# Attention scores from three narrower weight products, with the PSUM banks and the order of work rearranged around them

## The reference, cut to what matters

```python
qh = split_heads(x @ wq.T + bq, 16)          # 32 columns per head
kh = split_heads(ctx @ wk.T + bk, 16)        # 77 keys
vh = split_heads(ctx @ wv.T + bv, 16)
scores = einsum('ntd,nsd->nts', qh, kh) / sqrt(32) + mask * PAD
out = merge_heads(einsum('nts,nsd->ntd', softmax(scores), vh)) + x
out = (out - mean(out)) / sqrt(var(out) + 1e-5) * gamma + beta
```

## Time and profile before

| | |
|---|---|
| runs | 1153.67, 1154.09, 1157.71 us, median 1154.09 |
| the profiled execution | 1157.28 us |
| its span, first to last instruction | 1155.5 us |
| mean granted TensorE clock | 0.988 of 2.4 GHz |
| phase two begins | about 132 us |
| one iteration of phase two | 31.2 us, from 531.66 to 562.9 |
| busy: PE, DVE, POOL, ACT | 97%, 71%, 67%, 53% |

### The profile page before, as it was taken

How to read it: one execution, slowest core, us unless ns; L and a number is a source line. 1 busy time by engine, 2 the same in 40 slices (tenths; PEclk the granted TensorE clock), 3 DMA queues, 4 the chain that set the end, 5 groups by cost and what they waited for, 6 DMA issues and landing times.

```text
span 1155.5 us, 25702 instructions
## 1 busy us (share of the span) xinstructions
PE 1123.1 (97%) x7541; PEld 1037.8 (90%) x7541; DVE 822.1 (71%) x1622; ACT 612.5 (53%) x1008; POOL 771.8 (67%) x667
## 2 busy tenths in 40 slices
PE   7899999999999999999999999999999999999994
PEld 7788789999999999999999999999999999999983
DVE  5776467777777777777777777777777777777786
ACT  3321254556566555555555656655555555565551
POOL 4999523677766676766667776667676666777465
PEclk9999999999999999999999999999999999999996
DMA  7745433233343444343344333344443334333223
GB/s 228 261 147 188 150 104 90 74 122 95 116 119 117 126 126 126 116 120 99 102 123 122 106 105 119 117 126 126 126 116 122 98 102 123 123 101 110 85 82 128
DMA packets 147207, 141.07 MB, mean 122 GB/s; under 512 B 86452, under 2 KB 88004, under 8 KB 147172
## 3 DMA queue, kind: packets, MB, share of 16 engines
q1 hardware_dynamic: 146564, 140.29, 40.1%
q10 hardware_dynamic: 608, 0.33, 0.1%
HBM read 91.71 MB, written 48.85 MB: 122 GB/s over the span
## 4 chain that ended last, share of the span: by engine, by line
PE 84%; DVE 2%; POOL 1%; issue 0%; ACT 0%; DMA 0%; DVEq 0%; SPq 0%; POOLq 0%
PE q_ps L724 31%; PE o_ps L765 23%; PE s_ps L740 18%; PE t_ps L751 12%; POOL x_lo L991 0%; DVE stats L822 0%; DVE attn L853 0%; PE q_ps L765 0%; DVE y L862 0%; DMA xT_raw<-in_xT 0%; DVE attn L814 0%; DVE row_max L885 0%; DVE y L868 0%; ACT q_hi L1030 0%; DVE y L843 0%
## 5 line engine op out<-in xcount | busy, mean ns | idle before, releaser
L765 PE MATMUL o_ps<-v_tiles,pt 128*128 128x66 f32 x2520 | 310.7, 270 | 1.5 <-DVE attn L814 1.5
L765 PEld LDWEIGHTS o_ps<-v_tiles,pt 128*128 128x128 f32 x2520 | 304.0, 192 | 1.9 <-issue 1.9
L885 DVE TENSOR_REDUCE row_max<-s_ps 128x8 f32<-128x616 f32 x256 | 203.2, 794 | 118.2 <-PE s_ps L740 118.1
L740 PE MATMUL s_ps<-bd,q_hi 128*128 128x308 f32 x1024 | 260.5, 305 | 1.1 <-ACT q_hi L1030 1.1
L991 POOL TENSOR_TENSOR x_lo<-xT_raw,x_hi 128x512 fp32r<-128x512 f32 x124 | 159.3, 1286 | 117.8 <-ACT x_hi L1026 117.7
L961 POOL TENSOR_TENSOR attn<-attn,x_rows 128x512 f32<-128x512 f32 x124 | 160.2, 1292 | 115.8 <-DVE attn L814 115.8
L1036 ACT COPY pt<-t_ps 128x512 f32<-128x512 f32 (+1 forms) x320 | 175.0, 588 | 107.1 <-PE t_ps L751 107.0
L1030 ACT ACTIVATE q_hi<-q_ps,bq_col 128x512 fp32r<-128x512 f32 x125 | 86.1, 689 | 254.9 <-PE q_ps L724 254.9
L724 PE MATMUL q_ps<-x_lo,wq_hi 128*128 128x512 f32 x500 | 218.7, 437 | 2.5 <-PEq L142 2.1
L1016 ACT ACTIVATE probs<-probs 128x616 f32<-128x616 f32 x256 | 183.3, 716 | 64.3 <-DVE probs L894 64.3
L894 DVE TENSOR_TENSOR probs<-s_ps,row_max 128x616 f32<-128x616 f32 x256 | 204.6, 799 | 5.7
(11 more groups left out here) (96 smaller groups left out, 1292.9 us busy)
## 6 DMA issues: line engine op xcount, KB each, us to landing
xT_raw<-in_xT SPq DMA_DIRECT2D x128, 256.0 KB, 3.5
x_rows<-in_x SPq DMA_DIRECT2D x32, 1024.0 KB, 5.6
out<-y SPq DMA_DIRECT2D x128, 256.0 KB, 2.1
k_scratch<-k_out SPq DMA_DIRECT2D x8, 1232.0 KB, 5.4
bd<-k_scratch SPq DMA_DIRECT2D x128, 77.0 KB, 2.4
v_scratch<-v_out SPq DMA_DIRECT2D x16, 264.0 KB
v_tiles<-v_scratch SPq DMA_DIRECT2D x256, 9.9 KB
ctx_raw<-in_ctxT SPq DMA_DIRECT2D x3, 1232.0 KB, 6.2
```

What stands on the lines that cost most here:

```text
L740: mm = pe.matmul(s_ps[t % 2][:, j, 0:GS], (q_hi, q_lo)[u][:, g, P * t:P * t + P], bd[par][:, v, g, :, :].rearrange("p h s -> p (h s)"), st ...
L765: mm = pe.matmul(bank_of(b, t)[:, col:col + tile_cols[i]], pt[h][0:w, i, P * t:P * t + P], v_tiles[v_buffer(b, h)][0:w, i, 0:tile_cols[i]] ...
L885: dve.tensor_reduce(row_max[:, u, :].rearrange("p (j h) -> p j h", j=2), score_heads(t), AX.X, ALU.max).then_inc(max_ready, 1)
```

## The change

The score block of four heads is split otherwise. A head needs three terms, so four heads have twelve blocks of 32 rows by 77 keys. They are now packed into three weights of four row groups each: `q_a` holds the high part of heads 0, 1, 2 and again of head 0; `q_c` the low part of heads 0, 1, 2 and the high part of head 1; `q_b` the rest, of heads 2 and 3. Each head has 78 columns (77 and one of padding), so `q_a` and `q_c` meet 3 x 78 = 234 columns (`k_ac`), `q_b` 2 x 78 = 156 (`k_b`). There are still six score matmuls in a step. For that:

- Q's high part is two activations of ScalarE (96 and 64 rows), its low part two instructions of VectorE (96 and 32 rows); three DMAs on ScalarE's queue (`move_q`) copy Q's rows to other partitions, once for two groups.
- Keys are loaded by twelve DMAs for each batch, before by four.
- Q is made one step earlier (`q_of_step`) and has two PSUM banks; turns have one bank, and their order is 0 after the scores of tile step 0, 1 before and 2 after those of step 1, 3 and 4 after those of steps 2 and 3.
- VectorE makes Q's low part at the end of a step, in even steps. ScalarE does the exponential first, then Q, copies, x, normalizations. The quarters of x are split in steps 3, 4, 5 and 7.
- In phase one ScalarE copies the first half's keys of chunk 0 before the high part of chunk 1 and the `keep_v` tiles; KS, the number of key buffers, is 5, before 6; `keep_rows` lies in `v_out`. Gamma and beta are loaded at the start of phase two, where VectorE and GpSimd wait for them.

```diff
-    KDMA = HG * DMA
+    KDMA = 3 * HG * DMA
+    QDMA = 3 * DMA
-    KS = 6
+    KS = 5
+    SW = S + 1
+    QW = 3 * DH
...
                 for c in range(CHUNKS):
+                    if c == 0:
+                        keys(0, 0)
                     if c + 1 < CHUNKS:
                         high(c + 1)
-                    keys(c, 0)
+                    if c == 0:
+                        act.wait_ge(keep_turned, 1)
+                        for j in range(VT):
+                            act.copy(keep_v[0:v_n[j], j, :], v_ps[3][0:v_n[j], HEADS * j:HEADS * j + HEADS]
+                                     ).then_inc(keep_v_ready, 1)
+                    else:
+                        keys(c, 0)
...
-            t_ps = [ps(two, f"t_ps{i}", [P, BANK]) for i in range(2)]
-            q_ps = ps(two, "q_ps", [P, BANK])
+            t_ps = ps(two, "t_ps", [P, BANK])
+            q_ps = [ps(two, f"q_ps{i}", [P, BANK]) for i in range(2)]
+            X_STEPS = (3, 4, 5, 7)
-            TURNS = ([], [0, 1], [2, 3], [4])
+            TURNS_AHEAD = ([], [1], [], [])
+            TURNS_BEHIND = ([0], [2], [3], [4])
+            def q_of_step(s):
+                half, u = (s + 1) // 4, (s + 1) % 4
+                return (half + 1) // 2, (0 if half == 1 else 2) + u // 2, u % 2
...
                     at_least(sp, scores_done, b * 8 - 8)
-                    for q in range(HG):
-                        rows = slice(DH * q, DH * q + DH)
-                        sp.dma_start(bd[par][rows, :, :, q, :].bitcast(F32), k_dram[b, rows, :, :, :]
+                    for ac in range(2):
+                        for h in range(3):
+                            rows = slice(DH * h, DH * h + DH)
+                            sp.dma_start(k_ac[par][rows, ac, :, h, 0:S].bitcast(F32), k_dram[b, rows, 0, :, :]
+                                         ).then_inc(k_loaded[par], DMA)
+                        rows = slice(DH * ac, DH * ac + DH)
+                        sp.dma_start(k_ac[par][QW:P, ac, :, ac, 0:S].bitcast(F32), k_dram[b, rows, 1, :, :]
                                      ).then_inc(k_loaded[par], DMA)
+                    for q in range(2):
+                        sp.dma_start(k_b[par][DH * q:DH * q + DH, :, 1, 0:S].bitcast(F32), k_dram[b, QW:P, 0, :, :]
+                                     ).then_inc(k_loaded[par], DMA)
+                        rows = slice(DH * (q + 2), DH * (q + 2) + DH)
+                        sp.dma_start(k_b[par][rows, :, q, 0:S].bitcast(F32), k_dram[b, rows, 1, :, :]
+                                     ).then_inc(k_loaded[par], DMA)
+                sp.dma_start(gamma_all[:], gamma.partition_broadcast(P)).then_inc(scale_loaded, DMA)
+                sp.dma_start(beta_all[:], beta.partition_broadcast(P)).then_inc(scale_loaded, DMA)
...
+                    pe.wait_ge(q_moved[h], (b + 1) * QDMA)
                     for j in range(2):
                         g = 2 * h + j
-                        for n, (u, v) in enumerate(terms):
-                            mm = pe.matmul(s_ps[t % 2][:, j, 0:GS], (q_hi, q_lo)[u][:, g, P * t:P * t + P],
-                                           bd[par][:, v, g, :, :].rearrange("p h s -> p (h s)"),
-                                           start=(n == 0), stop=(n == 2))
+                        for ac, q in ((0, q_a), (1, q_c)):
+                            pe.matmul(s_ps[t % 2][:, j, 0:3 * SW], q[:, g, P * t:P * t + P],
+                                      k_ac[par][:, ac, g, :, :].rearrange("p h s -> p (h s)"),
+                                      start=(ac == 0), stop=False, skip_group_check=True)
+                        mm = pe.matmul(s_ps[t % 2][:, j, 2 * SW:GS], q_b[:, g, P * t:P * t + P],
+                                       k_b[par][:, g, :, :].rearrange("p h s -> p (h s)"),
+                                       start=False, stop=True, skip_group_check=True)
                     mm.then_inc(scores_done, 1)
...
                     pe.wait_ge(exp_done, b * 8 + (4 * h + 4))
-                    at_least(pe, pt_ready, b * (2 * NT) + (NT * h + i - 1))
+                    at_least(pe, pt_ready, b * (2 * NT) + (NT * h + i))
...
                         if real(a):
                             subtract_max(a, h, t)
+                        ahead, g, part = q_of_step(s)
+                        if part == 1 and real(a + ahead) and not in_phase_one(a + ahead, g):
+                            q_low(a + ahead, g)
...
-                        if 3 <= s <= 6 and real(a + 2):
-                            split_x(a + 2, s - 3, par)
+                        if s in X_STEPS and real(a + 2):
+                            split_x(a + 2, X_STEPS.index(s), par)
...
+                def move_q(b, h):
+                    act.wait_ge(q_hi_ready, b * 8 + (4 * h + 4))
+                    g = slice(2 * h, 2 * h + 2)
+                    act.dma_start(q_a[QW:P, g, :].bitcast(F32), q_a[0:DH, g, :].bitcast(F32)).then_inc(q_moved[h], DMA)
+                    act.dma_start(q_c[QW:P, g, :].bitcast(F32), q_a[DH:2 * DH, g, :].bitcast(F32)
+                                  ).then_inc(q_moved[h], DMA)
+                    act.dma_start(q_b[0:DH, g, :].bitcast(F32), q_b[QW:P, g, :].bitcast(F32)).then_inc(q_moved[h], DMA)
```

More of the change, by code:

```diff
@@ L96, in xattn @@
         q_lo_ready = sem("q_lo_ready")
+        q_moved = [sem(f"q_moved_{i}") for i in range(2)]
         x_hi_ready = sem("x_hi_ready")
@@ L251, in _ @@
                 sp.wait_ge(k_loaded[0], KDMA)
-                sp.wait_ge(consts_loaded, 3 * DMA)
+                sp.wait_ge(consts_loaded, DMA)
                 for half in range(2):
@@ L581, in xattn @@
             x_rows = sb(two, "x_rows", [P, TT, D], F32)
+            gamma_all = sb(two, "gamma_all", [P, D], F32)
+            beta_all = sb(two, "beta_all", [P, D], F32)
             attn = [sb(two, f"attn{i}", [P, TT, D], F32) for i in range(2)]
@@ L772, in step @@
                         h, t = s // 4, s % 4
-                        qb = a + h
-                        g = (2 if h == 0 else 0) + t // 2
-                        if real(qb) and not in_phase_one(qb, g):
-                            q_half(qb, g, t % 2, (par + h) % 2)
-                        if real(a):
-                            scores(a, h, t, par)
+                        ahead, g, part = q_of_step(s)
+                        if real(a + ahead) and not in_phase_one(a + ahead, g):
+                            q_half(a + ahead, g, part, (par + ahead) % 2)
                         last_turns = is_last(a - 1) and h == 0
@@ L784, in step @@
                         if real(a - 1 + h):
-                            for i in TURNS[t]:
+                            for i in TURNS_AHEAD[t]:
+                                turn(a - 1 + h, 1 - h, i)
+                        if real(a):
+                            scores(a, h, t, par)
+                        if real(a - 1 + h):
+                            for i in TURNS_BEHIND[t]:
                                 turn(a - 1 + h, 1 - h, i)
@@ L949, in step @@
                             subtract_max(a, h, t)
+                        ahead, g, part = q_of_step(s)
+                        if part == 1 and real(a + ahead) and not in_phase_one(a + ahead, g):
+                            q_low(a + ahead, g)
                         if s == 1 and real(a - 2) and not is_last(a - 2):
                             row_factors(a - 2)
+                dve.wait_ge(scale_loaded, 2 * DMA)
                 steps(dve, step)
@@ L985, in _ @@
                 pool.memset(minus_half[:], -0.5).then_inc(half_set, 1)
+                pool.wait_ge(scale_loaded, 2 * DMA)
                 pool.wait_ge(half_set, 1)
@@ L1035, in copy_pt @@
                     w = tile_rows[i]
-                    act.copy(pt[h][0:w, i, :], t_ps[(NT * h + i) % 2][0:w, :]).then_inc(pt_ready, 1)
+                    act.copy(pt[h][0:w, i, :], t_ps[0:w, :]).then_inc(pt_ready, 1)
                 def norm(b, t, par):
```

139 lines of the change are left out of this document (82 added, 57 removed).

## The result

The changed kernel takes 1284.03 us (median, 1278.2 to 1289.83) beside 1155.89 for the kernel before: ratio 1.111, interval 1.104 to 1.118, 128 us more. Forecast: 1297, the kernel before being at 1154.1 and 142.5 on top of it.

What follows compares the result with a forecast made beforehand. TensorE, busy 97% of the span, was taken as the bound. Loss of 4.85 us in each of 27 batches (131), plus 2, minus 3, plus 9 and 3.5, gave 142.5 on 1154.1: 1297 us, range 1186 to 1360.

Steps and rivals of the forecast that it cites:

- rival A: Loop: late y row and twelve key DMAs delay the values; products wait 4.1 us, clock loses 1.6 per batch; chance 0.62.
- Rival C: Loop: values land in time, so only scores and copies count; 1141 us; chance 0.10.
- the two delays: SyncE's queue: y's row 3.1 us later and keys 3.9 more, against a slack of 3.1.
- the wait: Step 4 of every batch: TensorE's product waits 4.1 us for the last value.
- The clock: Behind each wait of 4.1 us in the loop: granted clock falls to 0.50, losing 1.6 us.
- B: Loop: the same wait for values without the lower clock; with the rest 1252 us; chance 0.17.
- The moved rows: Loop: Q's moved parts take 5.2 us, 2.4 of it to land, hidden before scores 7.2 us later.
- the mark: Loop: a moved row of Q landing 2 us later would be seen.
- The narrow scores: Score matmuls in each step: weight loads hold each at 0.112 us; a step's scores fall from 0.85 to 0.67.
- One bank for turns: Loop: turn 2 waits 0.3 us for ScalarE's copy of turn 1, twice per batch, 0.6.
- Phase one and the start: Before the loop: key copies ahead of the high part cost 9 us; gamma, beta and two low parts 3.5.

Runs made afterwards that it cites:

- e1: The changed kernel with y's second row stored one iteration later, behind the values of the second half, in SyncE's queue: 1179.41 us, ratio 1.0203.
- e5: The kernel before with its keys loaded by twelve DMAs instead of four, the same bytes: 1156.83 us, ratio 1.0006.
- e10: The kernel before with x's last quarter split in step 7 instead of step 6, its four key DMAs kept: 1156.19 us, ratio 1.0002.
- e9: The kernel before with both twelve key DMAs and x's last quarter split in step 7: 1178.28 us, ratio 1.0204.
- e7: e4 with GpSimd doing y's row (a-3, 3) in step 3 before the split of x, not after it: 1153.82 us, ratio 1.0003.
- e12: e3 with ScalarE's high part of x at the head of its step, as in the kernel before: 1210.8 us, ratio 1.0476.
- e8: e7 with turn 1 before Q's matmuls in steps 1 and 5, not between Q and the scores: 1151.16 us, ratio 0.9967.
- e13: e8 with VectorE doing Q's two low parts after the inverse and the scaling of the product before: 1147.81 us, ratio 0.9931.
- e4: e1 with ScalarE's phase-one order of the kernel before, and gamma and beta waited for at first use: 1173.46 us, ratio 1.0158.
- e3: The changed kernel with x's last quarter split in step 6 again instead of step 7: 1283.83 us, ratio 1.1137.

## Why the prediction held, point by point

**The values (rival A): right.** The chain y row, keys, x, values, products is the one that sets the end; e1 removes 105 of 128 us by it, and e5, e10 and e9 show that neither delay costs by itself. Rival C fell as it was argued: the two delays together exceed the slack. The row was done at 4.1 into step 0, forecast 4.2, and for the reasons given.

**Its size: too large in the loop, too small at the start, so that part of the total is luck.** Up to the scores of iteration 3 the changed kernel loses 19.2 us, forecast 10 (9 and 3.5, less 0.85 for each of three batches). Over the 27 batches it loses 100.2, forecast 131. Behind them it is 2.2, forecast 1. The profiled spans differ by 121.6, forecast 142.5; the medians by 128.

The term that was mis-sized in the loop is the wait, 2.6 and not 4.1: the keys took 0.51 each and not 0.60, 1.05 us less, and without its waits the product would have started at 18.3 into the batch and not at 17.8 (20.74 less 2.42). A batch without the queue's wait is 0.65 shorter than before (e7), forecast 0.85. With 1.7 for the clock that makes 3.65 of the 3.71.

**The clock: A, not B.** From 239 to 1185 us the granted clock is 0.95, where the kernel before has 1.00, which is some 1.7 us a batch, forecast 1.6. But it isn't behind each wait: the clock fell in 20 of the 27 batches, in seven of them for twice as long as in the batch shown (as from 646 to 652.7). And the wait isn't one of 4.1: it is 1.76 plus 0.66 in one batch, 1.32 plus 1.49 in the next. That the average came out is luck in part.

**The moved rows: "hidden" was wrong in the changed kernel.** The sum took 2.4 us to land; beside x, which comes late behind the keys, they need 5.7 (median), and the scores wait up to 2.2. The prediction gave that as the mark (2 us later would be seen). It costs little of its own here, since in each of the 27 batches the product waits too, a few matmuls later. In e12 it is the larger of the two waits. With the keys early (e1, e7) the moved rows hold up nothing in the loop from iteration 4 to 29. No run took the moved rows away alone, so their price isn't measured.

**The narrow scores: right.** The changed kernel's scores start 0.11, 0.11 and 0.08 apart, then 0.14:

```profile
591.97 0.27 PE L793 MATMUL s_ps<-k_ac,q_a 128*128 128x234 f32 x1
592.08 0.28 PE L793 MATMUL s_ps<-k_ac,q_c 128*128 128x234 f32 x1
592.19 0.24 PE L796 MATMUL s_ps<-k_b,q_b 128*128 128x156 f32 x1
592.27 0.31 PE L793 MATMUL s_ps<-k_ac,q_a 128*128 128x234 f32 x1
```

A step takes 0.63 (591.97 to 592.60), forecast 0.67. The matmul of 156 columns was followed 0.08 later, less than the 0.112 taken as the floor of a load. The period without the queue's wait is 30.64 (e7), forecast 30.45. The estimate of 0.59 for a step was worked out from the 81 ns that the Trainium skill, "TensorE: Matmul & The Clock Gate", section "Back-to-back issue gap", gives for a matmul of 128 columns with its load. The 0.63 here lies between that estimate and the forecast; the 0.08 behind the matmul of 156 columns is as short as the page's 81 ns.

**One bank for turns: right in kind.** Turn 2 waited 0.20 (its scores ended at 616.48, it started at 616.68), 0.3 forecast; e8 and e13 win back part of it and of VectorE's low parts.

**ScalarE's queue: a term that was left out.** The prediction counted ScalarE's work ("ScalarE 2.4 more and six DMA issues") and not its order. High parts of x moved from the head of a step to its end, behind three issues that hold ScalarE 1.94 us. That cost 0.55 per batch where the queue is free (31.19 in e1, 30.64 in e7; 19.6 us from e4 to e7). In the changed kernel itself it has no share in the late row that a trace shows; ScalarE's order changed alone, with the split left in step 7, wasn't run.

**Phase one and the start: the sum was met, its parts were not.** TensorE's first matmul of phase two is 11.9 later (144.26 for 132.33), forecast 12.5. Phase one ends 9.7 later, forecast 9: GpSimd's last value tile is at 135.18 for 125.45. The fifth tile is 8.65 later, and the rest comes behind it, with TensorE at a granted clock of 0.50 from 46 to 52, where the kernel before has 0.57 from 38 to 42. The start adds 2.2 and not 3.5, and not for gamma and beta (e4): GpSimd waits 0.48 for beta, TensorE's first matmul not at all. What ends last before it is the third of ScalarE's DMA issues of phase one, at 143.29; before, it was VectorE's low part, at 131.75. Behind the first matmul another 7.3 us are lost by iteration 3, some 11 by iteration 4 in e7, which the prediction didn't have and whose cause stays open.

## What to carry to other kernels

Add up all delays ahead of one in-order queue's deadline: two changes that are free alone (1156.8 and 1156.2) cost 22.6 us together, because they spend one slack of 3.4 us. When an operation is moved, move what feeds it too, or nothing is won (e3, then e12). DMA issues on a compute engine are work on that engine: count them as instructions in its order, and ask who waits for what stands behind them. When one transfer comes later, look at which others it will then run beside (the moved rows: 2.4 us, then 5.7).

## What was not expected of the hardware

Three DMA issues on ScalarE keep it from its next operation for 1.94 us (0.51, 0.61 and 0.61 and the gaps). A DMA from SBUF to SBUF of 128 KB that lands in 2.3 to 2.4 us took 3.1 to 6.6, median 5.7, beside 1 MB of x. After waits of 1.76 and 0.66 us with the scores and a turn between them, the granted clock was 0.50 from 612 to 615; the prediction had put it behind one wait of 4.1.
